# Weight-times-value products with both value halves side by side, and row sums taken by ScalarE, in the first half of a decoder-layer kernel

## What is computed

```python
x = x + attn(layernorm(x))               # 16 heads of 64, ternary weights, RoPE, causal softmax, output projection
x = x + cross(layernorm(x), ctx, ctx)    # 16 heads of 64, causal softmax, no projections
x = x + moe(layernorm(x))                # top 1 of 8 low-rank experts
```

## Time and profile before

| | |
|---|---|
| runs shown | 2292.83, 2296.44, 2299.60 us |
| profiled execution, its own time | 2300.67 us |
| its span, first to last instruction | 2298.9 us |
| mean granted TensorE clock | 0.964 |
| busy: TensorE, VectorE, ScalarE, GpSimd | 2065.8, 1686.5, 1173.2, 994.8 us |
| 18-product group of L115 in both halves | 4608 products |
| exponentials (L105) in both halves | 1024, 428.4 us |

### The profile page before, as it was taken

One profiled execution on the slowest core, in us unless ns is written; L12 is line 12 of the kernel. 1 busy time (PEld: TensorE's weight loads), 2 busy tenths in 40 slices (PEclk: granted clock), 3 DMA queues, 4 the chain that ended last, 5 costly groups with the idle time before them and its releaser, 6 DMA issues. The chain is left out here.

```text
span 2298.9 us, 51989 instructions
## 1 busy us (share of the span) xinstructions
PE 2065.8 (90%) x19320; PEld 1332.1 (58%) x19320; DVE 1686.5 (73%) x4595; ACT 1173.2 (51%) x3114; POOL 994.8 (43%) x920
## 2 busy tenths in 40 slices
PE   1566899999999999999999999997789889998988
PEld 1344566666666666666666666665355545555544
DVE  8998777777777787777777777766466666767664
ACT  6786533443433333344333333434676767777761
POOL 5343333333343343333333333423565656565651
PEclk9777899999999999999999999998899999999989
DMA  8867656656556656556565566668999999999862
GB/s 234 181 152 150 127 127 145 150 125 158 134 134 146 143 130 158 134 141 151 124 159 138 138 139 143 127 156 205 233 192 233 197 216 211 219 212 217 198 137 74
DMA packets 800571, 372.82 MB, mean 162 GB/s; under 512 B 746552, under 2 KB 746808, under 8 KB 800320
## 3 DMA queue, kind: packets, MB, share of 16 engines
q1 hardware_dynamic: 800320, 369.50, 70.6%
HBM read 104.11 MB, written 49.28 MB: 67 GB/s over the span
## 5 line engine op out<-in xcount | busy, mean ns | idle before, releaser
L105 ACT ACTIVATE prob<-prob,negmax 128x128 f32<-128x128 f32 (+1 forms) x1024 | 428.4, 444 | 191.7 <-DVE negmax L98 191.3
L900 POOL TENSOR_TENSOR halves<-prob,halves 128x384 f16<-128x384 f32 x256 | 238.5, 932 | 579.6 <-ACT halves L824 579.6
L68 PE MATMUL ps_j<-xT,wT 128*128 128x256 f16 x3634 | 416.7, 275 | 21.9 <-DMA wT<-rows_qkv 21.9
L98 DVE CUSTOM_DVE_ANT_0 prob<-ps_s,mask 128x128 f32<-128x128 f32 (+1 forms) x1024 | 304.5, 353 | 169.2 <-PE ps_s L88 168.8
L68 PEld LDWEIGHTS ps_j<-xT,wT 128*128 128x128 f16 x3634 | 358.8, 99 | 82.9 <-issue 22.2
L1059 DVE TENSOR_TENSOR raw<-raw,cos 128x512 f32<-128x512 f32 x128 | 134.6, 1052 | 248.4 <-DMA swp<-raw 248.4
L813 ACT ACTIVATE raw<-ps_j,factor_qk 128x256 f32<-128x256 f32 x158 | 66.1, 469 | 446.1 <-PE ps_j L68 446.1
L1579 POOL TENSOR_TENSOR halves<-prob,halves 128x768 f16<-128x768 f32 x128 | 210.5, 1644 | 175.2 <-ACT halves L1529 175.2
L68 PE MATMUL ps_t<-xT,wT 128*128 128x256 f16 x2254 | 256.0, 274 | 0.0
L68 PEld LDWEIGHTS ps_t<-xT,wT 128*128 128x128 f16 x2254 | 221.5, 98 | 36.7
L68 PE MATMUL ps_j<-wT,yT 128*128 128x512 f16 x897 | 205.0, 384 | 0.0
(11 more groups left out here) (195 smaller groups left out, 3665.7 us busy)
## 6 DMA issues: line engine op xcount, KB each, us to landing
swp<-raw SPq DMA_DIRECT2D x512, 64.0 KB, 2.0
xin<-in_x SPq DMA_DIRECT2D x33, 512.0 KB, 4.5
kv_ahead<-in_ctx SPq DMA_DIRECT2D x16, 1024.0 KB, 6.4
x_kept<-after_self_attention SPq DMA_DIRECT2D x16, 1024.0 KB, 5.6
xres<-in_x SPq DMA_DIRECT2D x31, 512.0 KB, 4.4
after_self_attention<-xres SPq DMA_DIRECT2D x30, 512.0 KB, 3.2
queries<-q2T SPq DMA_DIRECT2D x30, 512.0 KB, 3.1
out<-x SPq DMA_DIRECT2D x10, 1024.0 KB, 4.6
```

Source lines behind the costliest of these rows:

```text
L68: last = pe.matmul(out, lhs(t[0], a), rhs(t[1], a), start=a == 0 and t is terms[0], stop=a == n_tiles - 1 and t == (0, 0))
L98: dve.tensor_tensor_reduce(scores[:, cols], bank[:, cols], hidden, scale, NO_SCORE, ALU.add, ALU.min, least[:, n:n + 1]).then_inc(done, 1)
L105: last = act.activation(prob[:, cols], prob[:, cols], ACT.Exp, scale=-1.0, bias=least[:, n:n + 1], accum_out=None if sums is None else sum ...
L900: pool.tensor_tensor(halves[:, e, 1, :], prob[:, e], halves[:, e, 0, :], ALU.subtract).then_inc(prob_lo, 1)
```

## The change

`weights_times_halves` takes the place of `weights_times_values` in the first half. The high half of the probabilities (index 0) meets both halves of the values in one product of 128 columns, which lands in two sides of 64 columns: side 0 has high x high and side 1 has high x low. The low half of the probabilities then meets the high values, 64 columns, added to side 0. It is 12 products a step, and `ps_o` fills its bank: heads x blocks x 2 sides x 64. The 65th column of `v` goes. The row sums come from the exponentials (`psums`, two slots). The two sides are added outside TensorE: ScalarE copies side 1 to `y` (`second_side`), VectorE adds side 0 (`o_added`, which frees the bank), then multiplies by the reciprocal. `second_side(g-2)` stands on ScalarE behind `probabilities(g-1)` and behind `scaled_rows`.

```diff
+def weights_times_halves(pe, out, pT, v, h):
+    for q, blocks in ((0, ((0, 0),)), (1, ((1, 0), (2, 1)))):
+        for b, kt in blocks:
+            pe.matmul(out[:, q], pT(0, b), v[:, :, kt, h, :], start=kt == 0, stop=False)
+            last = pe.matmul(out[:, q, 0, :], pT(1, b), v[:, 0, kt, h, :],
+                             start=False, stop=b == blocks[-1][0])
+    return last
...
-    ps_o = ps_ob[:, 0:2 * NT * PVW].rearrange("p (e n d) -> p e n d", e=2, n=NT)
+    ps_o = ps_ob[:].rearrange("p (e n i d) -> p e n i d", e=2, n=NT, i=2)
...
-    v = sb("v", [P, 2, NT, H, HD + 1], F16)
+    v = sb("v", [P, 2, NT, H, HD], F16)
+    psums = sb("psums1", [P, 2, 2, NT])
...                                                    # TensorE, weighted_sums
-                    pe.wait_ge(y_done, g)
+                    pe.wait_ge(o_added, g)
...
-                    last = weights_times_values(pe, ps_o[:, e],
+                    last = weights_times_halves(pe, ps_o[:, e],
...                                                    # ScalarE, probabilities
-                    exponentials(act, prob[:, e], negmax[:, e]).then_inc(exp_done, 1)
+                    if g > 1:
+                        act.wait_ge(recip_done, g - 1)
+                    exponentials(act, prob[:, e], negmax[:, e], psums[:, g % 2, e]) \
+                        .then_inc(exp_done, 1)
...
+            def second_side(g):
+                act.wait_ge(o_ready, g + 1)
+                if g > 1:
+                    act.wait_ge(y_lo, g - 1)
+                act.activation(y[:, g % 2].rearrange("p n (e d) -> p e n d", e=2),
+                               ps_o[:, :, :, 1, :], ACT.Copy).then_inc(side_out, 1)
...                                                    # ScalarE's loop, behind probabilities,
...                                                    # scaled_rows(1) and factor_rows
+                if 0 <= g - SUMS < GP:
+                    second_side(g - SUMS)
...                                                    # GpSimd: two memsets of v go, 6 -> 4 in zeroed
...                                                    # VectorE, normalised
-                dve.reciprocal(rinv[:], ps_o[:, :, :, HD]).then_inc(recip_done, 1)
-                if g > 1:
-                    dve.wait_ge(y_lo, g - 1)
+                dve.reciprocal(rinv[:], psums[:, g % 2]).then_inc(recip_done, 1)
+                z = y[:, g % 2].rearrange("p n (e d) -> p e n d", e=2)
+                dve.wait_ge(side_out, g + 1)
+                dve.tensor_tensor(z, ps_o[:, :, :, 0, :], z, ALU.add) \
+                    .then_inc(o_added, 1)
                 dve.wait_ge(recip_done, g + 1)
-                dve.tensor_tensor(
-                    y[:, g % 2].rearrange("p n (e d) -> p e n d", e=2),
-                    ps_o[:, :, :, 0:HD], rinv[:].unsqueeze(3).broadcast_to([P, 2, NT, HD]),
-                    ALU.mult).then_inc(y_done, 1)
+                dve.wait_ge(o_added, g + 1)
+                dve.tensor_tensor(z, z, rinv[:].unsqueeze(3).broadcast_to([P, 2, NT, HD]),
+                                  ALU.mult).then_inc(y_done, 1)
```

More of the change, by code:

```diff
@@ L181, in self_attention @@
     swp = sb("swp", [P, 2, T])
-    v = sb("v", [P, 2, NT, H, HD + 1], F16)
+    v = sb("v", [P, 2, NT, H, HD], F16)
+    psums = sb("psums1", [P, 2, 2, NT])
+    sb("unused1", [P, 24])
     xh = sb("xh", [P, 2, D], F16)
@@ L410, in self_attention @@
         recip_done = sem("recip_done")
+        side_out = sem("side_out")
+        o_added = sem("o_added")
         y_done = sem("y_done")
@@ L734, in expert_transposes @@
                 last.then_inc(j_ready, 1)
-            pe.wait_ge(zeroed, 6)
+            pe.wait_ge(zeroed, 4)
             pe.wait_ge(consts_done, IDENT_DONE)
@@ L793, in high_values @@
                     act.wait_ge(o_ready, NPAIR * (b - 1) + 4 * (j % 2) + 4)
-                act.activation(v[:, 0, j // 2, bass.ts(j % 2, H // 2), 0:HD],
+                act.activation(v[:, 0, j // 2, bass.ts(j % 2, H // 2), :],
                                bank(c)[:].rearrange("p (h d) -> p h d", d=HD),
@@ L907, in _ @@
             pool.memset(minus_half[:], -0.5).then_inc(zeroed, 1)
-            pool.memset(v[:, 0, :, :, HD:HD + 1], 1.0).then_inc(zeroed, 1)
-            pool.memset(v[:, 1, :, :, HD:HD + 1], 0.0).then_inc(zeroed, 1)
-            pool.wait_ge(zeroed, 6)
+            pool.wait_ge(zeroed, 4)
             for n in range(len(made[-1])):
@@ L961, in ternary @@
                 if n == 0:
-                    dve.wait_ge(zeroed, 6)
+                    dve.wait_ge(zeroed, 4)
                 if n >= NS:
@@ L1025, in low_values @@
                 dve.tensor_tensor(
-                    v[:, 1, j // 2, heads, 0:HD],
+                    v[:, 1, j // 2, heads, :],
                     bank(c)[:].rearrange("p (h d) -> p h d", d=HD),
-                    v[:, 0, j // 2, heads, 0:HD], ALU.subtract).then_inc(freed(c)[0], 1)
+                    v[:, 0, j // 2, heads, :], ALU.subtract).then_inc(freed(c)[0], 1)
             def low_ahead(c):
```

## The result

The changed kernel takes 2394.84 us (median of 4 runs, 2391.95 to 2397.45), the kernel before 2298.02 us over the runs beside it. The ratio is 1.041, 95% interval 1.038 to 1.044: slower by 97 us. The profiled execution has a span of 2395.7 us against 2298.9.

What follows compares the result with a forecast made beforehand. TensorE's matmul stream was taken as the bound from 280 us, VectorE before. 2300.67 + 41 early + 57 steady = 2398.7, with the profiled execution 4.2 above the median: 2394 us, range 2332 to 2440.

Steps and rivals of the forecast that it cites:

- The bound: From 280 us TensorE's matmul stream sets the 11.25 us step; VectorE idles 2.1 us a step, before that VectorE sets the pace.
- m+3.2: Forecast's start of the old kernel's rotation on VectorE, in us after m, the start of the maxima.
- rival A: Steady part: VectorE's idle hides the wait and only the early part pays, 2333 us; chance 0.16.
- count of eight steps: Steady part: following a batch's eight uneven steps, rotation plus middle against TensorE's 11.21, gives 11.75 us a step.
- Step 1: TensorE's products: the group of 12 takes 0.53 us, a gain of 0.03 to 0.04 us a step, 4 us over 113 steps.
- Step 2: Row sums on ScalarE: accumulator reads add 0.17 us a head, 0.35 a step; bounds 0.1 and 0.75.
- Step 3: VectorE's addition waits for ScalarE's copy, so the rotation can't start before m+4.9; bounds m+4.5 and m+5.4.
- Step 4: VectorE's steady loop, wait, rotation and middle, exceeds TensorE's 11.21: step 11.75 us, 57 us lost over 113 steps.
- Step 5: Early steps 2 to 9: VectorE waits longer for ScalarE, 47.4 us less waits replaced, 41 us lost; bounds 28 and 50.
- B: Whole kernel not slower: ScalarE's copy lands in time, only the products count, 2292 or 2275 us; chance 0.05.
- C: Shared SBUF port: multiplication and later rotation meet more GpSimd work, rotation delayed by m+5.4 or more, 2444 us; chance 0.14.

Runs made afterwards that it cites:

- e3: The changed kernel without the accumulator output of the exponentials, row sums a constant 1 (output not normalised): 2346.94 us, ratio 1.0209.
- e1: The changed kernel with ScalarE's copy of the second side moved ahead of the exponentials of the same step, up to step 127: 2314.46 us, ratio 1.0066.
- e9: e1 with GpSimd computing only 32 of 384 low halves of a head's probabilities (output lacks most of that correction): 2301.04 us, ratio 0.9996.
- e11: The changed kernel with GpSimd computing only 64 of 1024 low halves of each normed tile and 16 of 128 of each y: 2321.49 us, ratio 1.0115.
- e4: The changed kernel with the copy of the second side ahead of the exponentials in steps 2 to 13 only: 2361.19 us, ratio 1.0269.
- e8: e1 without the accumulator output of the exponentials, row sums a constant 1 (output not normalised): 2301.39 us, ratio 1.0009.
- e10: The changed kernel with GpSimd computing only 32 of 384 low halves of a head's probabilities: 2386.61 us, ratio 1.0382.
- e6: e1 with 18 products of 64 columns instead of 12 products: 2319.82 us, ratio 1.0091.
- e2: The kernel before plus one VectorE wait, normalised(g-2) waiting for ScalarE's last fp16 copy of probabilities(g-1), no instruction added: 2308.72 us, ratio 1.0042.
- e5: The changed kernel with VectorE instead of ScalarE copying the second side: 2308.03 us, ratio 1.0039.
- e7: The kernel before with row sums taken by ScalarE's exponentials and 18 products of 64 columns, no second side: 2304.52 us, ratio 1.0024.

## Why the prediction was right

**The bound.** That two microseconds of idle on VectorE were the cover, and that they could be used up, holds. One figure was read from one step: I wrote that the rotation used to start at m+3.2. Its mean is m+4.27. The loop was added up from m+4.9 and not from the shift, so the sum doesn't contain the slip; rival A's argument (the rotation is moved 1.7 us, less than the 2.1 of idle) did. With the mean shift of 0.65 it looks stronger still, and yet it fails: idle time is no cover for a wait that ends later than the one it replaces, once the loop's sum is above TensorE's step. The slip also stands in my check that the count of eight steps gives 11.2 for the old m+3.2 to m+4.0: the old kernel starts later than that in the mean, so the check said less than I took from it.

**Step 1.** 0.52 us for a forecast 0.53; 57 ns for a 128-column product, as interpolated. Between the groups of 65 and of 256 columns my rows give 0.43 ns a column, (113 - 31)/191, where I wrote 0.41; it is less than 0.01 us on the group.

**Step 2.** The reads cost 0.31 us by e3, forecast 0.35.

**Step 3.** Forecast m+4.9, measured 4.92 in the mean. The multiplication from SBUF took 438 ns in the mean over 340 to 1600 us, so the slowdown that I had as the upper bound didn't come. It does come with the side first: over 400 to 1500 us it takes 617 ns in e1, where it runs beside GpSimd's low halves of the probabilities, and 445 in e9, where those are short.

**Step 4.** Rotation 4.54 forecast, 4.50 measured; step 11.75 forecast, 11.73 measured; steady loss 57 and 55.5. e11 shows that it is a loop of wait, rotation and middle against TensorE's 11.21, e4 that it stands apart from the early loss. My count of eight steps was less good away from its point: for m+4.5 it gave 11.45, and e3 at m+4.61 has 11.35. The terms of the rotation add up to 4.55, not 4.54.

**Step 5.** 41 us forecast, 34.3 measured. The waits are as long as I had them: those of steps 2 to 9 are 42.4 of the 50.4 us, the longest 7.5, and with the 0.53 us of the added pass in each of the eight they make 47, my sum. But more came back than the 6 us that I allowed. The scores were 36.9 us late at step 9, and 2.6 of it came back until step 11, where VectorE's wait for the last tile of weights is 1.4 us for 5.9: I had priced steps 10 to 12 at nothing, and they gave something back.

**What I left out.** The end of the first half. From the scores of pair 127 to the first scores of the second half it takes 3.1 us more than before in the changed kernel, 3.1 to 4.3 in e1, e3, e4, e8, e9, e10 and e11, and 6.0 in e6; in e2, e5 and e7, which have no `second_side`, 0.7 to 1.3 us. The last `second_side` calls stand behind the experts' copies on ScalarE, which is a likely cause; no run moved these calls alone. The other 4 us of the 7 are inside the second half, and kernels that are alike there differ as much; their cause stays open. The 7 us too much in step 5 and these 7 us cancel, and so it is luck that 2394 met 2394.84 more closely than its parts deserve.

**The range.** Its steady bounds of 15 and 95 aren't worked out anywhere; step 4 had given 23 and 107. And 28 + 15 above 2296 is 2339, not the 2332 that I wrote. The outcome is well inside either.

**The rivals.** A falls (steady loss 55.5, not 0), and B falls with the time itself. C said that the rotation, moved later, would meet more of GpSimd's work. It meets as much as before, not more: 4.50 us for 4.58. But what it meets matters: with most of it away (e11) the rotation is 3.26 us, and the steady loss is gone.

## What to carry to other kernels

An engine that works in order and sits idle two microseconds a step can take two more passes for little (e5, 9 us of 2299, of which some 5 come with the accumulator reads by e7), but a wait for an engine that itself works on what it has just made is a loop through both, and has to be added up as one: from the maxima to the next maxima, with everything between. Such a loop can be shortened at either end: at the wait (e1) or at the work in it (e11, though that run leaves out part of the computation). Put the helper's instruction ahead of the work that depends on the newest result, not behind it (80 us here, for a move of two lines). Count columns, not products: 18 of 65 and 12 of 128 and 64 differ by 0.04 us.

## What the runs showed of the hardware

Reading the accumulator of ScalarE costs 186 ns as an instruction (80.0 us for 429 over 340 to 1600 us) and, where a copy waits for it, 0.16 us a head in the chain (half of the 0.31 us between e3 and the changed kernel). With no wait of VectorE for ScalarE's copy it isn't free either: e7 is 0.24% slower than before, and e8 regains the 13 us that e1 has over it.

A VectorE product of two SBUF operands took 0.69 us alone and up to 2.61 beside GpSimd (967.66 above). With most of GpSimd's work on x and y away, the mean of the second product of the rotation fell from 1525 to 731 ns over 400 to 1500 us, and the rotation from 4.50 to 3.26 us: more than a quarter of it in the changed kernel is waiting for GpSimd.
